# Seven block products in place of eight, over part of the columns, in the middle token stages of a fused fp32 layer

## The chip, the cores and the metric

One core of one Trainium2 chip runs one program. The metric is the time of the whole program on the device, in microseconds. Runs of this kernel agree within about 0.15%.

## The reference, cut to what matters

```python
delta = lora_B @ lora_A * 0.5
normalized = (weight + delta).reshape(O, 16, 128) / exp(scale_log)
quantized = cb[searchsorted((cb[:-1] + cb[1:]) / 2, normalized)]     # 32 levels
w_eff = (quantized * scale).reshape(O, I) + delta                    # 2048 x 2048
y = x @ w_eff.T                                                      # x: 4096 tokens x 2048
r = y @ W_base.T + b_base
probs = softmax(y @ router_w.T); ax = y @ A_w.T
mixed = einsum(einsum(ax, cores), probs)
out = x + r + (mixed @ B_w.T) * 2.0
```

Everything is fp32. The kernel multiplies the two matrices first: G = w_eff.T @ [W_base.T | A_w.T | router_w.T] + identity, 2048 x 2072, and then x @ G.

## The kernel before, in words

**Tiling.** The 2048 rows of G are 16 blocks of 128, in four groups of four. For each group there is a weight stage, which makes the group's four blocks of G in SBUF, and then a token stage, which multiplies all 4096 tokens (32 tiles `t` of 128) with them and adds the result to `part[t]`, 128 x 2072, which lives in HBM between stages. Group 0 has its own startup; the last group (`LAST` = 3) already has a token stage of another form, with pairs of tokens and seven products of half-width blocks (`ORDER`, `prod`).

**Precision.** Each product is three matmuls: both operands are split into a high part, rounded to fp32r (ScalarE copies), and a low part, the rest (a subtraction). High x high, high x low and low x high are added up in PSUM.

**Token stages 0 to 2** (`chunk`, `product`, lines 969 to 971). Token tile `t` has five chunks `c` of 384, 384, 384, 512 and 408 columns, one PSUM bank each (`m0` to `m4`), 12 matmuls a chunk. In stages 1 and 2 VectorE adds each bank to `part` (`evacuate`, line 1407), and TensorE writes a bank again when the add of the token before is done. ScalarE rounds the token's x (`xh`, line 1185), GpSimd takes its low part (`xl`, line 1623), 512 columns, in three buffers. SP loads x and part and stores part (`load_x`, `load_part` line 667, `store_part` line 672), in three buffers of part.

**The background.** Beside this, the other engines quantize the weights of later groups, half a block `q` (128 x 1024) at a time, 24 levels `j` each (`unit`): ScalarE makes a uint8 mask (line 1131, five buffers), VectorE adds it to `acc` (line 1362) and closes with the clamp, a sum of two SBUF tensors (line 1366). Seven more masks go by ScalarE (line 1137) to GpSimd (lines 1592 and 1606), which also normalises before (lines 1569, 1572; the delta rows come by DMA at level 5, and level 8 uses them) and scales after (lines 1611, 1613). Then ScalarE and GpSimd split the half block into high and low part (line 1617).

**Order.** All engines walk the same list of events (`walk`); each takes the events that are its own, in order. `Background.levels` deals the levels out between the chunks, by the share of the stage that has passed. So whatever an engine waits for holds everything behind it in the list. Stage 1 does half blocks 18 to 23, stage 2 does 26 to 31; weight stage 2 does 24 and 25.

```python
for t in range(NT):
    for c in range(NCH):
        yield ("chunk", g, t, c)
        if c == 2 and t + 2 < NT:
            yield ("x_split", g, t + 2)
        yield from back.levels(until, min(1.0, (NCH * t + c + 1) / (NT * NCH - 7)), 2 * FIRST[g + 1])
```

Of the kernel before, what the change touches and what calls it, by code (L numbers as in the profile page):

```python
# [77 lines left out]
SECOND = (506, 4)  # L78

# [8 lines left out]
    *(f"k{r}" for r in range(RING)), "x0", "x1", "x2", "pi0", "pi1", "pi2", "po0", "po1", "po2",  # L88
# [29 lines left out]
class Background:  # L118
# [29 lines left out]
def weights_of(g, back):  # L148
# [6 lines left out]
    for s in range(NS):  # L155
# [6 lines left out]
        yield from back.levels(until, min(1.0, (s + 1) / (NS - 6)), 2 * FIRST[g])  # L162
# [15 lines left out]

def operand_steps(n, k):
# [47 lines left out]
def walk():  # L227
# [11 lines left out]
class Room:  # L239
    def __init__(self, nc, ctx):  # L240
# [15 lines left out]
        self.gh = [self.take(f"gh{k}", DX, F32R) for k in range(NMAX)]  # L256
        self.gl = [self.take(f"gl{k}", DX, F32R) for k in range(NMAX)]
# [42 lines left out]
        self.tmp = self.put("tmp", at_x[0], 1536)  # L300
        row, r0 = 4 * DX, raw[0]
# [34 lines left out]
        self.chain_a, self.chain_b = (self.m[2], self.m[1], self.pd), (self.m[4], self.m[3], self.m[0])  # L336

# [256 lines left out]
def sync_program(e, R, S, io, part, delta, out):  # L594
    def raw(q):
        b, h = q // 2, q % 2
        if q >= RAW:
            wait_consumed(e, S, q - RAW)
        e.dma_start(R.wr[raw_of(q)], io["w"][b][:, h * H:(h + 1) * H]).then_inc(S[f"w{raw_of(q)}"], 16)
# [34 lines left out]
    def weight(g, s):  # L634
# [3 lines left out]
        if g == LAST and s in GUEST_LAST:  # L638
            if s == 2:
                e.wait_ge(S["used"], NS * (LAST - 1))  # L640
# [1143 lines left out]
```

## Time and profile before

| | |
|---|---|
| median of 3 runs | 2352.81 us (2351.86 to 2354.84) |
| the profiled execution | 2352.95 us, span 2351.2 us |
| PE busy | 2281.0 us, 97%, 11778 matmuls |
| VectorE / ScalarE / GpSimd busy | 1846.1 / 1464.8 / 1288.8 us |
| chain that ended last | PE 91%, DVE 6% |
| HBM | 306.41 MB read, 151.13 MB written, 195 GB/s |

PE is TensorE, DVE VectorE, ACT ScalarE, POOL GpSimd, SP the queue that issues DMAs. A matmul's duration in the trace is from its start to its modelled end, and matmuls overlap, so the pace is read from the distance of two starts. Token stage 1 runs from 891.4 to 1253.7 us, token stage 2 from 1436 to 1798 us. In a row of the timeline, the first number is the start in us and the second the duration.

### The profile page before, as it was taken

Reading aid. Unit: us, or ns where it says so; the run is one execution under the profiler, and the core shown is the slowest. Engines: PE = TensorE matmul, PEld = TensorE weight load, DVE = VectorE, ACT = ScalarE, POOL = GpSimd, SP = SyncE. Lnnn points to the kernel's source line nnn. Section 1 sums busy time; section 2 is a strip of 40 time slices with the busy share of each in tenths; the row PEclk is TensorE's granted clock in tenths of the full one; section 3 lists DMA queues with packets and bytes.
Section 4 is the critical chain, followed back from the end, with each engine's and each line's share of the span. In section 5 each row is a group of like instructions: output and inputs, shape, how many; then the busy total and the mean of one; then the engine's idle time right before and its main releaser. Section 6 shows DMA issues by size and latency. Waiting matters only on the chain.

```text
span 2351.2 us, 31846 instructions
## 1 busy us (share of the span) xinstructions
PE 2281.0 (97%) x11778; PEld 2083.8 (89%) x11778; DVE 1846.1 (79%) x2363; ACT 1464.8 (62%) x1926; POOL 1288.8 (55%) x792
## 2 busy tenths in 40 slices
PE   3989899999999999999999999999999999999999
PEld 2445479999999989999999989999999999999998
DVE  8999998889978866777777976777775666777776
ACT  8999978889877655666665665666663665121221
POOL 6888846669764336666663335666662222232331
PEclk9999999999999999999999999999999999999999
DMA  6788854453334335676674334666666666556463
GB/s 210 262 284 280 312 199 164 164 176 136 145 134 133 116 98 190 230 240 226 221 243 149 115 102 162 227 232 228 241 204 208 186 195 202 206 200 235 189 225 153
DMA packets 133088, 459.63 MB, mean 195 GB/s; under 512 B 14098, under 2 KB 66898, under 8 KB 96082
## 3 DMA queue, kind: packets, MB, share of 16 engines
q1 hardware_dynamic: 132932, 457.59, 57.3%
q8 instruction: 93, 1.52, 0.2%
q14 instruction: 63, 0.52, 0.1%
HBM read 306.41 MB, written 151.13 MB: 195 GB/s over the span
## 4 chain that ended last, share of the span: by engine, by line
PE 91%; DVE 6%; ACT 2%; DMA 1%; issue 1%; DVEq 0%; SPq 0%; ACTq 0%
PE m L970 15%; PE m L969 15%; PE m L971 15%; PE m L926 5%; PE m L927 5%; PE m L925 5%; PE m L868 5%; DVE acc L1362 4%; PE m L1018 4%; PE m L1020 4%; PE m L1019 4%; PE m L956 2%; PE m L957 2%; PE m L958 2%; ACT mk L1131 1%; PE pd L1018 1%
## 5 line engine op out<-in xcount | busy, mean ns | idle before, releaser
L1362 DVE SCALAR_TENSOR_TENSOR acc<-mk,dj,acc 128x1024 f32<-128x1024 uint8 x736 | 945.4, 1285 | 102.8 <-ACT mk L1131 83.6
L1131 ACT ACTIVATE mk<-wr,bj 128x1024 uint8<-128x1024 f32 x736 | 809.0, 1139 | 1.0 <-DVE acc L1362 0.5
L970 PE MATMUL m<-gl,xh 128*128 128x384 f32 (+2 forms) x1920 | 674.1, 351 | 0.0
L969 PE MATMUL m<-gh,xh 128*128 128x384 f32 (+2 forms) x1920 | 673.5, 351 | 0.0
L971 PE MATMUL m<-gh,xl 128*128 128x384 f32 (+2 forms) x1920 | 671.6, 350 | 0.0
L1606 POOL TENSOR_TENSOR pp<-pp,tm 128x1024 f32<-128x1024 f32 x184 | 447.3, 2431 | 22.3 <-POOL tm L1592 0.6
L971 PEld LDWEIGHTS m<-gh,xl 128*128 128x128 f32 x1920 | 360.6, 188 | 18.0
L969 PEld LDWEIGHTS m<-gh,xh 128*128 128x128 f32 x1920 | 361.0, 188 | 17.2
L970 PEld LDWEIGHTS m<-gl,xh 128*128 128x128 f32 x1920 | 360.9, 188 | 16.9
L1592 POOL TENSOR_SCALAR tm<-mp,dj 128x1024 f32<-128x1024 uint8 x192 | 217.6, 1134 | 281.5 <-ACT mp L1137 276.3
L1413 DVE TENSOR_TENSOR kl<-kw,kh 128x416 fp32r<-128x416 f32 (+3 forms) x310 | 238.0, 779 | 104.9 <-ACT kh L1165 103.7
L1165 ACT ACTIVATE kh<-kw 128x416 fp32r<-128x416 f32 (+3 forms) x310 | 169.2, 549 | 220.0 <-DMA kw<-in_wb 125.8
L1407 DVE TENSOR_TENSOR part<-m,part 128x384 f32<-128x384 f32 (+2 forms) x320 | 188.1, 588 | 139.0 <-PE m L971 138.3
L1137 ACT ACTIVATE mp<-wr,bj 128x1024 uint8<-128x1024 f32 x224 | 254.9, 1138 | 0.0
L925 PE MATMUL m<-kh,wh 128*128 128x384 f32 (+2 forms) x624 | 219.2, 351 | 0.0
L927 PE MATMUL m<-kh,wl 128*128 128x384 f32 (+2 forms) x624 | 218.6, 350 | 0.0
L926 PE MATMUL m<-kl,wh 128*128 128x384 f32 (+2 forms) x624 | 218.6, 350 | 0.0
L1185 ACT ACTIVATE xh<-xw 128x512 fp32r<-128x512 f32 x96 | 60.3, 630 | 253.2 <-DMA xw<-in_x 253.0
L868 PE MATMUL m<-rows,wr 128*128 128x384 f32 (+2 forms) x560 | 207.7, 534 | 2.7 <-DMA rows<-in_wb 2.2
L868 PEld LDWEIGHTS m<-rows,wr 128*128 128x128 f32 x560 | 112.5, 201 | 96.7 <-issue 51.3
L1454 DVE TENSOR_TENSOR part<-m,part 128x346 f32<-128x346 f32 (+1 forms) x272 | 136.0, 515 | 63.5 <-PE m L1020 30.6
L1018 PE MATMUL m<-op,pxh 128*128 128x346 f32 (+1 forms) x544 | 178.8, 329 | 0.0
(198 smaller groups left out, 3363.7 us busy)
## 6 DMA issues: line engine op xcount, KB each, us to landing
part<-part SPq DMA_DIRECT2D x192, 1036.0 KB, 7.6
rows<-in_wb SPq DMA_DIRECT2D x61, 1036.0 KB, 4.8
out<-part SPq DMA_DIRECT2D x31, 1024.0 KB, 4.5
kw<-in_ws SPq DMA_DIRECT2D x128, 208.0 KB, 2.6
xw<-in_x SPq DMA_DIRECT2D x96, 256.0 KB, 3.4
kw<-in_wb SPq DMA_DIRECT2D x92, 192.0 KB, 2.4
wr<-in_w SPq DMA_DIRECT2D x32, 512.0 KB, 8.6
dl<-delta SPq DMA_DIRECT2D x30, 512.0 KB, 5.9
```

What stands on the lines that cost most here:

```text
L868: done = e.matmul(R.m[c][:, 0:width(c)], R.wr[raw_of(q)][:, (t % 8) * 128:(t % 8 + 1) * 128], R.rows[r % 3][:, cols(c)], start=t == 0, sto ...
L925: e.matmul(bank[:, 0:w], high, kh, start=t == 0, stop=False)
L926: e.matmul(bank[:, 0:w], high, kl, start=False, stop=False)
L927: done = e.matmul(bank[:, 0:w], low, kh, start=False, stop=t == NB - 1 and not own(b, c))
L969: e.matmul(R.m[c][:, 0:w], xh, gh, start=k == 0, stop=False)
L970: e.matmul(R.m[c][:, 0:w], xh, gl, start=False, stop=False)
L971: done = e.matmul(R.m[c][:, 0:w], xl, gh, start=False, stop=stop and k == n - 1)
L1018: e.matmul(bank, high, oh, start=kp == 0 and n in (1, 2, 5), stop=False, skip_group_check=n in (3, 4, 6, 7))
L1131: e.activation(R.mk[m % NM], w, ACT.Identity, bias=R.bj[:, j:j + 1], scale=GROW).then_inc(S["mk"], 1)
L1137: e.activation(R.mp[k % 2], w, ACT.Identity, bias=R.bj[:, NV + i:NV + i + 1], scale=GROW).then_inc(S["mp"], 1)
L1362: e.scalar_tensor_tensor(R.acc, R.mk[m % NM], R.dj[:, j:j + 1], R.acc, ALU.mult, ALU.add).then_inc(S["ac"], 1)
L1606: e.tensor_tensor(R.pp, first, R.tm[scaled_level(q, i)], ALU.add).then_inc(S["pp"], 1)
```

## The change

It concerns token stages 1 and 2 (`MIXED`). The tokens are taken in 16 pairs. The first and the last pair keep their chunks; each of the 14 between is a list of 13 units (`MIX`). For the first 448 columns of each half of G (the halves are 1036 wide), the 2 x 2 block scheme of the last stage is used: two tokens by two halves of the group's rows, seven products of six matmuls of 448 columns in place of eight. The other 588 columns of each half are done as before, in three rest units a token of 392 columns, 12 matmuls each; the third takes 196 columns from each half. Products use two banks in turn, rest units the other four.

The products need sums: of G's blocks, once a stage, in pair 0 (`spread` on VectorE, eight operations of 896 columns, `spread_high` on ScalarE, `spread_low` on GpSimd), and of x, once a pair (`token_sums`, four sums of 256 columns, and `token_sums_low` on GpSimd, `token_sums_high` on ScalarE). x gets a fourth buffer. G's sums lie where `wh` was, so the half blocks of the next group are split into high and low part only in the last pair of the stage, half of the later groups' low parts on VectorE (`VECTOR_SPLITS`), and four of group 3 in its weight stage. Levels are dealt out by columns passed, none beside the first 6 units and the last 11, nor beside the first four slots of weight stage 2. The raw half block 24 is loaded in the last pair of stage 1, and normalised at its close. SP's loads and stores are issued at the events `fetch`, `more` and `half_done`. The rest of the kernel stays.

```diff
+SW = 448
+REST = (HX - SW) // 3 * 2
+MIX = (("prod", 1), ("prod", 2), ("rest", 0, 0), ("rest", 0, 1), ("prod", 6), ("prod", 5), ("rest", 0, 2), ("prod", 7),
+       ("prod", 3), ("rest", 1, 0), ("prod", 4), ("rest", 1, 1), ("rest", 1, 2))
+MIXED = (1, 2)
+MIX_FIRST, MIX_LAST = 1, PAIRS - 2
+NMIX = MIX_LAST - MIX_FIRST + 1
+SUM_SLOT = {4: 0, 6: 1, 5: 2, 3: 3}
+SPARE_RAW = {1: (3, 4, 2), 2: (0, 1, 10)}
+SPLITS = {1: tuple(range(8, 16)), 2: (16, 18, 20, 22, 17, 19, 21, 23), 3: (24, 26, 25, 27, 28, 29, 30, 31)}
+SPLIT_POS = {q: 8 * (g - 1) + k for g, qs in SPLITS.items() for k, q in enumerate(qs)}
+VECTOR_SPLITS = (17, 19, 21, 23, 25, 27)
+WAIT_LEVELS, END_LEVELS, WAIT_SLOTS = 6, 11, 4
+LATE_SPLITS = {20: 28, 24: 29, 28: 30, 32: 31}
...
-        if self.j % SPLIT_EVERY == SPLIT_EVERY - 1 and (self.q, self.j) > LAST_DELTA:
+        if self.j % SPLIT_EVERY == SPLIT_EVERY - 1 and (self.q, self.j) > LAST_DELTA and self.split < 2 * FIRST[2]:
...
-        yield from back.levels(until, min(1.0, (s + 1) / (NS - 6)), 2 * FIRST[g])
+        wait = WAIT_SLOTS if g - 1 in MIXED else 0
+        yield from back.levels(until, min(1.0, max(0, s + 1 - wait) / (NS - 6 - wait)), 2 * FIRST[g])
...
+def mixed_tokens_of(g, back):
+
+    until = UNTIL_TOKENS[g]
+    back.begin(until)
+    costs = [unit_columns(u) for u in UNITS_OF[g]]
+    unit = costs[0]
+    total, passed = sum(costs) - (WAIT_LEVELS + END_LEVELS) * unit, -WAIT_LEVELS * unit
+    for k, u in enumerate(UNITS_OF[g]):
+        p, at = u[0], k - PAIR_FIRST[g][u[0]]
+        yield ("mul", g, k)
+        if at == 0:
+            yield ("fetch", g, p)
+        if p == 0 and at in (0, 1, 2):
+            yield ("spread", g, at)
+        if p == 0 and at in (1, 2, 3, 4):
+            yield ("spread_high", g, at - 1)
+            yield ("spread_low", g, at - 1)
+        if p + 1 < PAIRS:
+            if at == 3:
+                yield ("x_split", g, 2 * p + 2)
+            if at == 4:
+                yield ("x_split", g, 2 * p + 3)
+                yield ("more", g, p)
+            if at == 5 and mixed(p + 1):
+                yield ("token_sums", g, p + 1)
+            if at == 6:
+                yield ("x_low", g, 2 * p + 2)
+            if at == 9 and mixed(p + 1):
+                yield ("token_sums_high", g, p + 1)
+                yield ("token_sums_low", g, p + 1)
+            if at == (10 if mixed(p) else 9):
+                yield ("x_low", g, 2 * p + 3)
+        elif at < 7:
+            if g + 1 < LAST or at < 4:
+                yield ("split", SPLITS[g + 1][at])
+        if at == (9 if mixed(p) else 5):
+            yield ("half_done", g, p)
+        if p == PAIRS - 1 and at == 6:
+            yield ("next_weights", g)
+        if p == PAIRS - 1 and at == 8:
+            yield ("next_rounded", g)
+        passed += costs[k]
+        yield from back.levels(until, min(1.0, max(0.0, passed / total)), 0)
+    yield ("close", g)
+    if g + 1 < LAST:
+        yield ("split", SPLITS[g + 1][7])
...
+def unit_bank(u):
+
+    if u[1] == "chunk":
+        return u[3]
+    if u[1] == "prod":
+        return 1 if u[2] in (2, 3, 5) else 0
+    return 2 + (6 * u[0] + 3 * u[2] + u[3]) % 4
+
+
+def unit_tokens(u):
+
+    if u[1] == "prod":
+        return (TARGET[u[2]][0],), {1: (0,), 2: (0,), 4: (1,)}.get(u[2], ())
+    return (u[2],), (u[2],)
...
-        for c in range(NCH):
-            wait_evacuated(e, S, g, t, c)
+        if g == 0:
+            for c in range(NCH):
+                wait_evacuated(e, S, g, t, c)
+        else:
+            e.wait_ge(S["ed"], added(g, last_unit(g, t, 0)))
...
+        elif what == "fetch":
+            g, p = at
+            if p + 1 < PAIRS:
+                load_x(g, 2 * p + 2)
+                load_x(g, 2 * p + 3)
+            if p:
+                store_part(g, 2 * p - 1)
+        elif what == "more":
+            g, p = at
+            if p:
+                load_part(g, 2 * p + 2)
+        elif what == "half_done":
+            g, p = at
+            store_part(g, 2 * p)
+            if p + 1 < PAIRS:
+                load_part(g, 2 * p + 3)
+            elif g == 1:
+                raw(2 * FIRST[LAST])
...
+            e.wait_ge(S["wl"], 8 if g == 1 else 12)
+        if s == 8 and g > 1:
+            e.wait_ge(S["wd"], 4)
...
+        if (kind, *at) == ("prod", 6):
+            e.wait_ge(S["ql"], sums_count(g, p))
+            e.wait_ge(S["bl"], 4 * g)
+        before = bank_before(g, k)
+        if before is not None:
+            e.wait_ge(S["ed"], added(g, before))
...
+        bank = (*R.m, R.pd)[unit_bank(UNITS_OF[g][k])]
+        if kind == "prod":
+            n = at[0]
+            for kp in range(2):
+                high, low = sum_factor(g, p, n, kp)
+                oh, ol = sum_operand(n, kp, False), sum_operand(n, kp, True)
+                e.matmul(bank[:, 0:SW], high, oh, start=kp == 0 and n in (1, 2, 5), stop=False, skip_group_check=n in (3, 4, 6, 7))
+                e.matmul(bank[:, 0:SW], high, ol, start=False, stop=False, skip_group_check=n in (3, 4, 6, 7))
+                done = e.matmul(bank[:, 0:SW], low, oh, start=False, stop=kp == 1, skip_group_check=n in (3, 4, 6, 7))
+        else:
+            u, i = at
+            _, xl, xh = R.token(g, 2 * p + u)
+            for b in range(GROUP[g]):
+                r = slice(b * 128, (b + 1) * 128)
+                gh, gl = rest_columns(R.gh[b], i), rest_columns(R.gl[b], i)
+                e.matmul(rest_bank(bank, i), xh[:, r], gh, start=b == 0, stop=False)
+                e.matmul(rest_bank(bank, i), xh[:, r], gl, start=False, stop=False)
+                done = e.matmul(rest_bank(bank, i), xl[:, r], gh, start=False, stop=b == GROUP[g] - 1)
+        done.then_inc(S["mc"], 1)
...
+    def token_sums_high(g, p):
+        e.wait_ge(S["qs"], 4 * sums_count(g, p))
+        if p > MIX_FIRST:
+            e.wait_ge(S["mc"], multiplied(g, prod_unit(g, p - 1, 3)))
+        elif g > 1:
+            e.wait_ge(S["used"], NS * g)
+        e.activation(R.sh[g], R.sf, ACT.Copy).then_inc(S["qh"], 1)
...
+    def mul_added(g, k):
+        p, kind, *at = UNITS_OF[g][k]
+        t = 2 * p + unit_tokens(UNITS_OF[g][k])[0][0]
+        part, bank = R.part[t % 3], (*R.m, R.pd)[unit_bank(UNITS_OF[g][k])]
+        if k == first_unit(g, t, 0):
+            e.wait_ge(S[f"pi{t % 3}"], slot_round(g - 1, t))
+        e.wait_ge(S["mc"], multiplied(g, k))
+        if kind == "chunk":
+            c = at[1]
+            to, of = part[:, cols(c)], bank[:, 0:width(c)]
+        elif kind == "rest":
+            to, of = rest_columns(part, at[1]), rest_bank(bank, at[1])
+        else:
+            first = HX * TARGET[at[0]][1]
+            to, of = part[:, first:first + SW], bank[:, 0:SW]
+            before = target_before(g, k)
+            if before is not None:
+                e.wait_ge(S["ed"], added(g, before))
+        e.tensor_tensor(to, of, to, ALU.add).then_inc(S["ed"], 1)
+
+    def split(q):
+        e.wait_ge(S["wh"], SPLIT_POS[q] + 1)
+        e.tensor_tensor(R.wl[raw_of(q)], R.wr[raw_of(q)], R.wh[high_of(q)].bitcast(F32), ALU.subtract).then_inc(S["wd"], 1)
+
+    def spread(g, k):
+        br, r, f, n = S["br"], R.sum_raw, R.sum_f, 8 * (g - 1)
+
+        def rebuilt(to, i, h):
+            e.tensor_tensor(grouped(r[to], 2), both_blocks(R.gah, i, h).bitcast(F32), both_blocks(R.gal, i, h).bitcast(F32),
+                            ALU.add).then_inc(br, 1)
+
+        if k == 0:
+            e.wait_ge(S["used"], NS * g)
+            e.wait_ge(S["lo"], NCH * FIRST[g + 1])
+            rebuilt(1, 0, 1)
+            rebuilt(0, 0, 0)
+            e.wait_ge(br, n + 2)
+            e.tensor_tensor(f[0], r[1], r[0], ALU.subtract).then_inc(br, 1)
+        elif k == 1:
+            rebuilt(2, 1, 1)
+            e.wait_ge(br, n + 4)
+            e.tensor_tensor(f[1], r[2], r[1], ALU.subtract).then_inc(br, 1)
+            e.tensor_tensor(f[2], r[2], f[0], ALU.subtract).then_inc(br, 1)
+        else:
+            rebuilt(3, 1, 0)
+            e.wait_ge(br, n + 7)
+            e.tensor_tensor(f[3], r[3], f[2], ALU.subtract).then_inc(br, 1)
...
+    def spread_low(g, k):
+        e.wait_ge(S["bh"], 4 * (g - 1) + k + 1)
+        if k in (0, 2):
+            e.wait_ge(S["br"], 8 * (g - 1) + (6 if k == 0 else 8))
+        e.tensor_tensor(R.sum_l[k], R.sum_f[k], R.sum_h[k].bitcast(F32), ALU.subtract).then_inc(S["bl"], 1)
+
+    def token_sums(g, p):
+        n, x = 4 * (sums_count(g, p) - 1), [R.token(g, t)[0] for t in (2 * p, 2 * p + 1)]
+        a11, a12, a21, a22 = (quarter(x[k // 2], 0, k % 2) for k in range(4))
+        s1, s2, s3, s4 = (grouped(R.sf[:, 256 * k:256 * (k + 1)], 2) for k in range(4))
+        for t in (2 * p, 2 * p + 1):
+            e.wait_ge(S[f"x{x_buffer(g, t)}"], x_landed(g, t))
+        if n:
+            e.wait_ge(S["ql"], n // 4)
+        if p == MIX_FIRST:
+            e.wait_ge(S["used"], NS * g)
+        e.tensor_tensor(s1, a21, a22, ALU.add).then_inc(S["qs"], 1)
+        e.tensor_tensor(s3, a11, a21, ALU.subtract).then_inc(S["qs"], 1)
+        e.wait_ge(S["qs"], n + 1)
+        e.tensor_tensor(s2, s1, a11, ALU.subtract).then_inc(S["qs"], 1)
+        e.wait_ge(S["qs"], n + 3)
+        e.tensor_tensor(s4, a12, s2, ALU.subtract).then_inc(S["qs"], 1)
+
+    def token_sums_low(g, p):
+        e.wait_ge(S["qh"], sums_count(g, p))
+        e.tensor_tensor(R.sl[g], R.sf, R.sh[g].bitcast(F32), ALU.subtract).then_inc(S["ql"], 1)
```

## Rows read from the trace of the kernel before

**Rows 1.** Windows: token stage 1; granted clock, DMA share, GB/s last.

```profile
891.40:1253.70 362.30, 362.30 (x1923) 345.20 (x1922) 275.98 (x314) 218.98 (x228) 243.67 (x141) 1.00 0.66 222
```

**Rows 2.** Waits, 895 to 1250 us: total us, times, longest.

```profile
DVE part L1407 <- PE m L971: 68.4, 120, 2.2
...
POOL wr L1569 <- DMA dl<-delta: 6.3, 4, 3.4
```

**Rows 3.** Timeline of PE, stage 1: first matmul of each run of one width.

```profile
999.66 0.40 PE L969 MATMUL m<-gh,xh 128*128 128x512 f32 x1
...
1002.45 0.34 PE L969 MATMUL m<-gh,xh 128*128 128x408 f32 x1
...
1004.68 0.34 PE L969 MATMUL m<-gh,xh 128*128 128x384 f32 x1
...
1010.97 0.40 PE L969 MATMUL m<-gh,xh 128*128 128x512 f32 x1
```

**Rows 4.** Timeline of PE, last stage: 17 intervals of 344 or 346 columns.

```profile
2101.27 0.32 PE L1018 MATMUL m<-op,pxh 128*128 128x346 f32 x1
...
2103.94 0.32 PE L1020 MATMUL m<-op,psl 128*128 128x346 f32 x1
```

**Rows 5.** Tile ps, last stage: GpSimd sums, and their low part.

```profile
L1639 POOL TENSOR_TENSOR ps<-px x16: 726/738/1098, 1918.3 to 2308.6; 128x256 f32<-128x256 f32 x16
...
L1655 POOL TENSOR_TENSOR psl<-ps,pxh x16: 2382/2394/2403, 1939.5 to 2314.5; 128x1024 fp32r<-128x1024 f32 x16
```

**Rows 6.** Groups by form, 895 to 1250 us, VectorE: busy us, mean ns.

```profile
L1362 DVE SCALAR_TENSOR_TENSOR acc<-mk,dj,acc 128x1024 f32<-128x1024 uint8 x138 | 176.9, 1282 | 14.1 <-ACT mk L1131 13.9
...
L1407 DVE TENSOR_TENSOR part<-m,part 128x384 f32<-128x384 f32 x95 | 52.8, 556 | 28.9 <-PE m L971 28.5
...
L1407 DVE TENSOR_TENSOR part<-m,part 128x512 f32<-128x512 f32 x31 | 21.4, 692 | 27.8 <-PE m L971 27.8
...
L1366 DVE TENSOR_TENSOR wr<-acc,pp 128x1024 f32<-128x1024 f32 x6 | 7.3, 1225 | 0.6
```

**Rows 7.** Timeline of VectorE, stage 1: level, add, level.

```profile
1100.73 1.29 DVE L1362 SCALAR_TENSOR_TENSOR acc<-mk,dj,acc 128x1024 f32<-128x1024 uint8 x1 [0.59 <-ACT mk L1131]
1101.93 0.55 DVE L1407 TENSOR_TENSOR part<-m,part 128x384 f32<-128x384 f32 x1
1102.40 1.28 DVE L1362 SCALAR_TENSOR_TENSOR acc<-mk,dj,acc 128x1024 f32<-128x1024 uint8 x1
```

**Rows 8.** Groups by form, 895 to 1250 us, GpSimd: low parts.

```profile
L1623 POOL TENSOR_TENSOR xl<-xw,xh 128x512 fp32r<-128x512 f32 x30 | 38.9, 1298 | 29.8 <-ACT xh L1185 29.7
...
L1617 POOL TENSOR_TENSOR wl<-wr,wh 128x1024 fp32r<-128x1024 f32 x7 | 16.9, 2412 | 1.0 <-ACT wh L1148 1.0
```

**Rows 9.** Timelines of VectorE, then GpSimd, weight stage 1.

```profile
763.20 2.12 DVE L1413 TENSOR_TENSOR kl<-kw,kh 128x384 fp32r<-128x384 f32 x1 [0.56 <-ACT kh L1165]
...
773.12 1.27 DVE L1362 SCALAR_TENSOR_TENSOR acc<-mk,dj,acc 128x1024 f32<-128x1024 uint8 x1
...
762.39 2.52 POOL L1606 TENSOR_TENSOR pp<-pp,tm 128x1024 f32<-128x1024 f32 x1
...
772.95 2.52 POOL L1606 TENSOR_TENSOR pp<-pp,tm 128x1024 f32<-128x1024 f32 x1
```

**Rows 10.** By line, 895 to 1250 us: store_part (L672), load_part (L667).

```profile
DMA to landing us min/median/max: 4.6/9.3/10.7
...
DMA to landing us min/median/max: 5.2/7.1/8.8
```

**Rows 11.** DMA issues, 895 to 1250 us: median us to landing last.

```profile
xw<-in_x SPq DMA_DIRECT2D x29, 256.0 KB, 3.4
dl<-delta SPq DMA_DIRECT2D x6, 512.0 KB, 9.3
```

**Rows 12.** Groups by form, 895 to 1250 us, ScalarE: masks, high parts of tokens.

```profile
L1131 ACT ACTIVATE mk<-wr,bj 128x1024 uint8<-128x1024 f32 x137 | 148.6, 1135 | 0.0
...
L1185 ACT ACTIVATE xh<-xw 128x512 fp32r<-128x512 f32 x30 | 19.0, 632 | 124.8 <-DMA xw<-in_x 124.8
```

More of the change, by code:

```diff
@@ L444, in wait_final_row, with mixed, units_of_stage, unit_columns @@
         e.wait_ge(S[f"f{k}"], 16)
+def mixed(p):
+    return MIX_FIRST <= p <= MIX_LAST
+def units_of_stage():
+    units = []
+    for p in range(PAIRS):
+        if mixed(p):
+            units += [(p, *u) for u in MIX]
+        else:
+            units += [(p, "chunk", u, c) for u in range(2) for c in range(NCH)]
+    return units
+def unit_columns(u):
+    if u[1] == "prod":
+        return 6 * SW
+    return 12 * (REST if u[1] == "rest" else width(u[3]))
+def unit_bank(u):
[4 more added lines that the diff above has]
+    return 2 + (6 * u[0] + 3 * u[2] + u[3]) % 4
@@ new lines, in last_unit, with first_unit, prod_unit, multiplied @@
+def last_unit(g, t, reads):
+    return max(k for k, u in enumerate(UNITS_OF[g]) if u[0] == t // 2 and t % 2 in unit_tokens(u)[reads])
+def first_unit(g, t, reads):
+    return min(k for k, u in enumerate(UNITS_OF[g]) if u[0] == t // 2 and t % 2 in unit_tokens(u)[reads])
+def prod_unit(g, p, n):
+    return PAIR_FIRST[g][p] + MIX.index(("prod", n))
+def multiplied(g, k):
+    return MC_BASE[g] + k + 1
+def added(g, k):
+    return ED_BASE[g] + k + 1
+def bank_before(g, k):
+    return max((j for j in range(k) if unit_bank(UNITS_OF[g][j]) == unit_bank(UNITS_OF[g][k])), default=None)
@@ new lines, in target_before, with sums_count, sums_free, x_buffer @@
+def target_before(g, k):
+    p, kind, *at = UNITS_OF[g][k]
+    same = [j for j in range(PAIR_FIRST[g][p], k) if UNITS_OF[g][j][1] == "prod" and TARGET[UNITS_OF[g][j][2]] == TARGET[at[0]]]
+    return max(same, default=None)
+def sums_count(g, p):
+    return NMIX * (g - 1) + p - MIX_FIRST + 1
+def sums_free(g):
+    return multiplied(g, prod_unit(g, MIX_LAST, 3))
+def x_buffer(g, t):
+    return t % 4 if g in MIXED else t % 3
+def x_landed(g, t):
+    if g == 0:
+        return 16 * (t // 3 + 1)
+    k = t % 4
+    return 16 * ((PER_SLOT[k] if k < 3 else 0) + NT // 4 * (g - 1) + t // 4 + 1)
@@ L447, in wait_evacuated, with x_released, rest_columns, rest_bank @@
+def x_released(g, k):
+    if g == 0:
+        return NCH * (3 * (PER_SLOT[k] - 1) + k + 1)
+    return multiplied(g, last_unit(g, NT - 4 + k, 1))
+def rest_columns(t, i):
+    if i < 2:
+        return t[:, HX * i + SW:HX * i + SW + REST]
+    return halves(t)[:, :, SW + REST:HX]
+def rest_bank(bank, i):
+    return bank[:, 0:REST] if i < 2 else halves(bank[:, 0:REST])
+def both_blocks(t, i, h):
+    return t.rearrange("p (a i n) -> p a i n", a=2, i=2)[:, :, i, HX * h:HX * h + SW]
 def wait_evacuated(e, S, g, t, c):
-    if g == 0 and c in ACT_CHUNKS:
+    if g in MIXED:
+        e.wait_ge(S["ed"], added(g, PAIR_FIRST[g][t // 2] + NCH * (t % 2) + c))
+    elif c in ACT_CHUNKS:
@@ L639, in weight @@
             if s == 2:
[L640 removed]
+                e.wait_ge(S["mc"], sums_free(2))
             elif s == 3:
@@ L802, in sync_program @@
                     weight(g + 1, s)
+        elif what == "fetch":
[16 more added lines that the diff above has]
+                raw(2 * FIRST[LAST])
+        elif what == "next_weights":
+            for s in range(RING):
+                weight(at[0] + 1, s)
         elif what == "close":
@@ L1084, in tensor_program @@
             chunk(*at)
+        elif what == "mul":
+            mul(*at)
         elif what == "prod":
@@ L1294, in scalar_program @@
                 weight(g + 1, 1)
+        elif what == "next_rounded":
+            weight(at[0] + 1, 0)
+            weight(at[0] + 1, 1)
+        elif what == "spread_high":
+            spread_high(*at)
+        elif what == "token_sums_high":
+            token_sums_high(*at)
         elif what == "close":
@@ L1709, in gpsimd_program @@
         elif what == "split":
-            split(*at)
+            if at[0] not in VECTOR_SPLITS:
+                split(*at)
         elif what == "slot":
```

157 lines of the change are left out of this document (123 added, 34 removed), and 3 rows, old and new, of the table COMPUTE.

## The prediction

> **What bounds the kernel now.** I read the windows by stage first, then the waits of a token stage, then the timeline of PE. Token stage 1 lasts 362.3 us with TensorE busy throughout; VectorE is busy 276.0 us, ScalarE 219.0, GpSimd 243.7 [rows 1]. Who waits says the same: VectorE waited 68.4 us for matmuls, and GpSimd 6.3 us for delta rows [rows 2]; no wait of TensorE is in that view. A busy PE isn't yet a PE at its pace, so the starts are read: 12 matmuls of 512 columns in 2.79 us, 12 of 408 in 2.23, 36 of 384 in 6.29 [rows 3], that is 0.2325, 0.186 and 0.1747 us each. A token takes 11.31 us, a pair 22.62, for 49,728 columns: 0.4549 ns a column, with next to nothing per instruction. Sixteen pairs make 361.9 us, so a token stage is its matmul columns and nothing else. That is where a saving of columns counts in full, as long as the other engines keep up.
>
> **TensorE's part.** A mixed pair has 7 products of 6 matmuls x 448 columns (18,816) and 6 rest units of 12 x 392 (28,224): 47,040 columns, 2,688 fewer, at 0.4549 ns = 1.22 us; the pair takes 21.40 us. 14 pairs in 2 stages: 28 x 1.22 = **34.2 us off**. Could the narrower matmul be held by its weight load? In the last stage 18 successive matmuls of 344 or 346 columns start over 2.67 us, 0.157 from one to the next [rows 4], under the 0.178 of 392 columns, so no. The third rest unit reads two runs of 196 columns; no row shows such a matmul. From below it costs nothing more; from above, as two of the 0.157 us just seen, 0.136 us x 24 x 28 = 91 us. I take nothing: GpSimd's sums read 128-element runs and take 0.738 us for 256 elements, in line with 2.394 for 1024 in one run [rows 5].
>
> **VectorE's part.** An add of 384 took 556 ns, of 512 692 [rows 6]; between them 448 gives 0.624 and 392 0.565. A pair has 7 x 0.624 + 6 x 0.565 = 7.76 us of adds, before 5.9. The background stays 144 levels a stage (6 half blocks x 24), at 1.282 us, with 6 clamps at 1.225 [rows 6], but now has less time: the stage has 14 x 47,040 + 2 x 49,728 = 758,016 columns, and none is issued beside the first 6 units or the last 11 of 4,608 columns, which leaves 679,680 columns, 309 us: 9.95 levels a pair. So 7.76 + 9.95 x 1.282 + 0.41 x 1.225 = 21.0 us of durations in 21.40. They overlap: an add starts 1.20 us after a level of 1.29, a level 0.47 after an add of 0.55 [rows 7], some 0.085 for each of 23 instructions: 2.0 us. Real load 19.0, spare **2.4 us** a pair. From this go the old waits for masks (13.9 of the 14.1 us ahead of the levels [rows 6], 0.9 a pair) and a new one: ScalarE rounds the next sums only when product 3 is done (one buffer), at 13.74 us of the pair (6 products of 1.22 and 3 rest units of 2.14), needs 1.1 us for it and 1.1 for the mask behind it (a mask of that size takes 1.135 [rows 12]), while VectorE wants that mask at 14.6: 1.4 us. What is left is 0.1 us. It also must not be late: a product's bank is written again after one product and one rest unit (1.22 + 2.14 = 3.4 us), where a chunk's was after four chunks (some 9 us).
>
> **GpSimd's part.** Of 243.7 us, 32 token low parts at 1.298 and 8 weight low parts at 2.412 [rows 8] are 60.8; the other 183 us are the levels' share, 1.27 us each. A mixed pair needs 9.95 x 1.27 = 12.6, two token low parts 2.6, four sums at 0.738 and their low part at 2.394 [rows 5] 5.35: 20.6 of 21.4 us. Spare **0.8 us**, a 96% load. Its products are due some 12 us after they are issued, and an engine that is late no longer waits for its inputs, so I charge little. ScalarE gets one pass of 1024 a pair and keeps a third of its time.
>
> **The port.** In weight stage 1 a subtraction of two SBUF tensors on VectorE took 2.12 us in place of some 0.55 (its PSUM sister of the same width, [rows 6]): it began at 763.20 under a GpSimd add that ended at 764.91, and ended at 765.32. The mask step (uint8 mask and accumulator, both in SBUF) began at 773.12 under another GpSimd add and took 1.27 us as ever [rows 9]. So two-tensor subtractions and adds in SBUF wait for GpSimd, levels don't. New ones of the kind are the eight rebuilt sums of 896 in pair 0 and the low parts that move to VectorE; and the clamp, which found GpSimd idle, will now find it at work. Each may wait up to 2.4 us: the clamps 0.41 x 2.4, at most 1.0 and at the middle 0.5 us a pair. With them VectorE's load and waits are 21.8 us in 21.4: I let 0.2 us a pair reach TensorE, half of the excess, since a late VectorE finds its next masks ready and waits less; nothing and 0.9 us (with 1.0 for clamps) are the ends. The Trainium skill (SBUF — State Buffer, section SBUF: two separate sides) says that the pair of ports is an exclusive lock which an operation with two SBUF inputs and a GpSimd one take in turn, and that the loser fully blocks. The trace agrees for the subtraction and not for the mask step; what it would make of this change if it held for both is the last rival.
>
> **Pair 0 and the stage ends.** The eight sums at about 1.1 us (1.225 for 1024) are 8.7 us of VectorE, beside 5.9 of adds and 5 levels (6.4): 21.0 of 22.6 us, and their low parts 4 x 2.1 on GpSimd. TensorE first wants them 6.7 us into pair 1. Cost nothing; with waits at the port VectorE runs 2 to 7 us late there, against banks of 9 us. In pair 15 eight weight halves are split after the last level: on GpSimd 4 x 2.41 = 9.6 us behind its last normalising work, on VectorE 4 x 1.2. The GpSimd ones are due at slot 0, after 22.6 us; if it is over 8 us behind, TensorE waits the rest. Raw half block 24 is loaded there ahead of the first weights: I charge 1 us a stage. In weight stage 2 48 levels go into 70 slots in place of 74, 6% denser, with the low parts of the weights prepared three slots ahead: nothing.
>
> **SP's queue.** Per pair it still moves two parts in and two out, but in another order: the odd token's load waits, at the head of the queue, for the landing of the even token's store, and the next pair's loads of x stand behind it. The store goes out when unit 8 is added, at 13.74 + 0.2 + 0.63 = 14.6 us of the pair. Stores landed in 4.6 to 10.7 us, median 9.3, loads in 5.2 to 8.8, median 7.1 [rows 10], but those went out together with each other and with x. This store goes out alone, so I take 5 us: the load leaves at 19.6 and lands near 25 to 27, due at 30.8 (end of the sixth unit of the next pair). Then x (3.4 us [rows 11]) isn't late either. The delta rows for the next half block are asked for at level 5 and used at level 8, 6.5 us on, and take 9.3 [rows 11]; twice in six they fall behind that wait. This lands on GpSimd's 0.8 us, and its lateness hides part of it.
>
> **Sum.** -34.2 + 28 x 0.2 + 2 x 1 at the stages' ends = -26.6 us. The profiled execution took 2352.95 us (span 2351.2), 0.14 over the median of the runs shown: 2352.8 - 26.6 = 2326.2, say **2326 us**. Ends of this case: the whole 34.2, 2318.6, and 0.9 us a pair lost, 2346.
>
> **Rivals.** (a) *GpSimd becomes the bound.* If its waits for delta (6.3) and a like sum at other handovers stay beside a 96% load (spare 14 x 0.8 = 11 us a stage), levels finish late, clamps hold VectorE, and adds hold TensorE: some 5 to 10 us a stage, 2336 to 2346. For it: the load. Against: those waits were of an engine that had run ahead. (b) *The store is slow, and the change is slower.* With S us for the even token's store, x leaves at 14.6 + S, and the first mask behind it needs 3.4 us to land and 0.63 + 1.13 for x's high part and the mask [rows 12], due at 26.7 (the third unit's add of the next pair): VectorE stalls for S - 6.9. It has 2.4 us to spare and 1.2 were gained, so with no other wait the kernel loses from S = 10.5 on, and with the 1.4 us behind product 3 from 9.1 on; at the longest store seen, 10.7, that is 3.8 + 1.4 - 2.4 = 2.8 us x 28 - 34.2 = +44, 2397; at the median of 9.3, 1.4 x 28 - 34.2 = +5, 2358. For it: the median of 9.3. Against: nothing else large is in flight by then. (c) *VectorE's lateness isn't made up.* If the waits for masks, clamps and x add up in full and a level in progress delays adds past the 3.4 us of a bank, 1.2 us a pair go: 2353, no change. (d) *Levels block at the port too.* 12.8 us of levels and 20.6 of GpSimd in turn would take 33 us a pair, 28 x 12 = 330 us slower, 2650. By that rule token stage 1 would have had 176.9 + 243.7 us in 362, so it's all but excluded.
>
> **Chances.** Likeliest 0.62, (a) 0.18, (b) 0.11, (c) 0.08, (d) 0.01. 0.2% is 4.7 us, about what this kernel's runs can tell from no change. Faster: the first two, 0.80; same 0.08; slower 0.12. Range 2318 to 2347: it holds the likeliest case and (a), and leaves (b), (c) and (d) out.
>
> **What would show it.** Right: matmuls of 448 start 0.204 us apart, of 392 0.178, those with two runs as well; a token stage takes 345 to 351 us; TensorE's waits there stay under 6 us; VectorE busy 88% or more, GpSimd 93% or more inside the pairs. Wrong: matmuls of the first product units waiting for part, a wait of part or xh for DMA of microseconds in each pair, clamps of 3 us, a stage of 356 us or more, or the third rest unit above 0.2 us a matmul.

## The result and the profile after

The changed kernel took **2357.81 us** (median of 20 runs, 2354.79 to 2362.82), the kernel before 2352.65 on the same chip (20 runs, 2351.29 to 2356.02): a ratio of 1.0021, 95% interval 1.0015 to 1.0028. It is slower by 0.2%, where 2326 was forecast and 2318 to 2347 given. From the start of one stage's first matmul to the next stage's:

| us | before | after |
|---|---|---|
| startup and token stage 0 | 336.7 + 373.2 | 334.2 + 373.2 |
| weight stage 1, token stage 1 | 181.8, 362.0 | 181.7, **361.6** |
| weight stage 2, token stage 2 | 181.7, 362.0 | 182.3, **362.3** |
| weight stage 3, last token stage | 185.0, 368.9 | **189.0**, 369.2 |

By its columns a token stage would take 14 x 21.39 + 2 x 22.62 = 344.7 us. So the two stages gave back 16.9 and 17.6 us, all that 34.2 us of fewer columns had brought, and weight stage 3 lost 4.0 more. Of the profile's page, the share of each engine and the chain that ended last, of which PE was 91% before:

```profile
PE 2254.3 (96%) x11610; PEld 2061.6 (88%) x11610; DVE 1918.7 (82%) x2469; ACT 1496.8 (64%) x1962; POOL 1439.8 (61%) x934
...
PE 71%; DVE 8%; POOL 6%; DMA 6%; ACT 5%; issue 3%; SPq 0%; POOLq 0%; DVEq 0%; ACTq 0%
```

The windows of token stage 1 and of 912 to 1215 us in it, which holds pairs 1 to 13 (913.2 to 1206.7) and the start of pair 14 (us, then busy time and count of PE, weight loads, DVE, ACT, POOL, then clock, DMA share, GB/s), for [rows 1]:

```profile
891.40:1255.00 363.60, 349.15 (x1846) 334.11 (x1845) 307.85 (x368) 233.13 (x242) 315.36 (x210) 1.00 0.60 221
912.00:1215.00 303.00, 289.01 (x1526) 277.12 (x1527) 257.67 (x315) 207.16 (x213) 277.44 (x190) 1.00 0.63 232
```

TensorE, busy throughout before, now idles 14 us in this stage. In the pairs' window GpSimd is busy 277.4 of 303 us (92%) and VectorE 257.7 (85%): neither is full. The waits in that window (total, times, longest), for [rows 2]:

```profile
ACT sh L1503 <- POOL sf L2031: 50.2, 10, 8.0
DVE acc L1687 <- ACT mk L1435: 42.2, 23, 5.1
ACT xh L1491 <- DMA xw<-in_x: 33.3, 9, 7.7
PE m L1270 <- DVE part L1747: 12.8, 10, 2.5
ACT sh L1503 <- PE m L1272: 12.2, 3, 5.1
```

Where VectorE waited for TensorE, TensorE now waits for VectorE, at L1270, the first product of a pair. VectorE waits for masks, and ScalarE, which makes them, for GpSimd's sums of x (`sf`) and for x itself. One pair shows how these hang together. It starts at 1028.87, the next at 1052.10: 23.23 us in place of 21.39. Timelines of GpSimd, ScalarE, VectorE and TensorE:

```profile
1042.95 0.74 POOL L2026 TENSOR_TENSOR sf<-xw 128x256 f32<-128x256 f32 x1
...
1045.16 0.74 POOL L2031 TENSOR_TENSOR sf<-xw,sf 128x256 f32<-128x256 f32 x1
...
1037.91 2.18 ACT L1435 ACTIVATE mk<-wr,bj 128x1024 uint8<-128x1024 f32 x2
1045.93 1.06 ACT L1503 ACTIVATE sh<-sf 128x1024 fp32r<-128x1024 f32 x1 [5.84 <-POOL sf L2031]
1046.90 1.13 ACT L1435 ACTIVATE mk<-wr,bj 128x1024 uint8<-128x1024 f32 x1
...
1042.86 1.15 DVE L1747 TENSOR_TENSOR part<-m,part 128x448 f32<-128x448 f32 x2
1048.07 1.29 DVE L1687 SCALAR_TENSOR_TENSOR acc<-mk,dj,acc 128x1024 f32<-128x1024 uint8 x1 [4.07 <-ACT mk L1435]
...
1051.34 0.61 DVE L1747 TENSOR_TENSOR part<-m,part 128x448 f32<-128x448 f32 x1
...
1052.10 0.44 PE L1270 MATMUL m<-gh,xh 128*128 128x448 f32 x1 [1.60 <-DVE part L1747]
```

GpSimd comes to the four sums 14.1 us into the pair and ends them at 1045.90. ScalarE had reached the rounding at 1040.1 and stood 5.84 us; the mask behind it, which doesn't need the sums, came at 1048.0. VectorE stood 4.07 us for that mask, so it added the pair's last product, whose matmuls had begun at 1044.83, only at 1051.34; TensorE, which writes that bank first in the next pair, stood 1.60 us. Each engine hands on a part of its lateness.

### The profile page after: what moved, and what is told of

Its sections match the earlier page's. It is cut to its first block, busy times and chain, and to the rows that moved or that the text cites. A ratio compares the mean times of both kernels' runs of the same rounds, so it can differ in the third digit from the quotient of the medians.

```text
span 2353.6 us, 31902 instructions
## 1 busy us (share of the span) xinstructions
PE 2254.3 (96%) x11610; PEld 2061.6 (88%) x11610; DVE 1918.7 (82%) x2469; ACT 1496.8 (64%) x1962; POOL 1439.8 (61%) x934
## 4 chain that ended last, share of the span: by engine, by line
PE 71%; DVE 8%; POOL 6%; DMA 6%; ACT 5%; issue 3%; SPq 0%; POOLq 0%; DVEq 0%; ACTq 0%
PE m L1106 7%; PE m L1214 6%; PE m L1213 6%; PE m L1215 6%; PE m L1165 5%; PE m L1167 5%; PE m L1166 5%; DVE acc L1687 4%; PE m L1320 4%; PE m L1322 4%; PE m L1321 4%; ACT mk L1435 3%; DMA xw<-in_x 2%; PE m L1200 2%; PE m L1201 2%
## 5 line engine op out<-in xcount | busy, mean ns | idle before, releaser
L1781 DVE TENSOR_TENSOR kl<-kw,kh 128x416 fp32r<-128x416 f32 (+3 forms) x310 | 254.5, 833 | 97.0 <-ACT kh L1470 96.2
L1214 PE MATMUL m<-gl,xh 128*128 128x384 f32 (+2 forms) x800 | 280.9, 351 | 0.0
L1213 PE MATMUL m<-gh,xh 128*128 128x384 f32 (+2 forms) x800 | 280.6, 351 | 0.0
L1215 PE MATMUL m<-gh,xl 128*128 128x384 f32 (+2 forms) x800 | 279.8, 350 | 0.0
L1747 DVE TENSOR_TENSOR part<-m,part 128x448 f32<-128x448 f32 (+4 forms) x362 | 209.7, 591 | 22.5 <-PE m L1215 16.3
L1320 PE MATMUL m<-op,pxh 128*128 128x346 f32 (+1 forms) x544 | 178.9, 329 | 0.0
L1321 PE MATMUL m<-op,pxh 128*128 128x346 f32 (+1 forms) x544 | 174.2, 320 | 0.0
L1280 PE MATMUL m<-gl,xh 128*128 128x392 f32 x504 | 171.9, 341 | 0.0
L1279 PE MATMUL m<-gh,xh 128*128 128x392 f32 x504 | 171.9, 341 | 0.0
L1281 PE MATMUL m<-gh,xl 128*128 128x392 f32 x504 | 171.5, 340 | 0.0
```

What stands on the lines that cost most here:

```text
L1213: e.matmul(R.m[c][:, 0:w], xh, gh, start=k == 0, stop=False)
L1214: e.matmul(R.m[c][:, 0:w], xh, gl, start=False, stop=False)
L1215: done = e.matmul(R.m[c][:, 0:w], xl, gh, start=False, stop=stop and k == n - 1)
L1320: e.matmul(bank, high, oh, start=kp == 0 and n in (1, 2, 5), stop=False, skip_group_check=n in (3, 4, 6, 7))
L1321: e.matmul(bank, high, ol, start=False, stop=False, skip_group_check=n in (3, 4, 6, 7))
```

## The experiments

Three theories were set against each other. **H**, head of the line: `token_sums_high` stands too early in the common list, and ScalarE holds the masks while it waits for GpSimd's sums. **X**: the loads of x land late, and ScalarE's `xh` holds the masks. **G**: GpSimd's load is the bound, wherever things stand. The expectations name a fourth, **B**: the two banks of the products are written again too soon for a loaded VectorE. Each run was timed beside the kernel before on the same chip, and the brackets give the ratio to it with its interval; the edits are made to the changed kernel. Medians of different groups of runs were taken on different chips, where the kernel before took 2351.2 to 2353.9 us, so a difference of 2 or 3 us between such medians tells nothing by itself.

**Where the rounding stands.** `round11` moves the sums' rounding and their low part two units later, to unit 11; `round12` has 12 in its place; `round11_low9` moves the rounding alone.

```diff
-            if at == 9 and mixed(p + 1):
+            if at == (11 if mixed(p) else 9) and mixed(p + 1):
                 yield ("token_sums_high", g, p + 1)
                 yield ("token_sums_low", g, p + 1)
```

> The rounding of the next pair's sums (ScalarE) and their low part (GpSimd) go two units later, behind unit 11 instead of unit 9. Theory H (ScalarE is held: it stands in its order before the rounding until GpSimd's late sums are there, the masks behind it come late, VectorE's adds come late and TensorE waits for a bank at each pair's start): VectorE's waits for masks in the mixed pairs fall from 4 us a pair to under 2, and the program takes 2325 to 2338 us. Rival G (GpSimd's load of 96% is the bound whatever the order): within 5 us of 2357. Rival B (two banks for products are reused too soon for a loaded VectorE): within 5 us of 2357.

> Only ScalarE's rounding of the sums goes behind unit 11; GpSimd's low part stays at its old place behind unit 9, so GpSimd may stand for ScalarE. Theory H: still faster than the change, 2325 to 2345 us, since ScalarE runs ahead of VectorE and reaches the rounding before GpSimd, which is late, gets to the low part. Rival G: within 5 us of 2357. Rival B: the same. If it is slower than the kernel with both moved, GpSimd's waits for ScalarE count.

> Rounding and low part both behind unit 12, the pair's last. Theory H: the mask side is as good as behind unit 11 or better, but the low part is due at the fifth unit of the next pair, 6.7 us later, and a GpSimd that is 6 us late makes TensorE wait for it: 2328 to 2350 us, with waits of product 6 for the low part of the sums in the trace. Rival G and rival B: within 5 us of 2357.

Measured: **2342.23** (0.9954, 0.9937 to 0.9971), **2343.32** (0.9962, 0.9947 to 0.9977) and **2351.49** (0.9995, 0.9985 to 1.0004). The place of the rounding is worth 15.6 us, with no less work for GpSimd and the same banks, so H holds and neither G nor B is the whole cause; the low part's own place doesn't count. H alone asked for more: 2342.23 lies above its 2325 to 2338, though VectorE's waits for masks did fall from 3.2 us a pair to 1.8. At unit 12, just above the 2350 expected, most of the gain is lost again. The product that needs the sums is the fifth unit of the next pair, and TensorE's waits for their low part rise from 3.9 us in round11 to 7.1 over the two stages, as expected; in the traces these stages are 2.0 and 1.8 us longer, and the rest of the 9.3 us isn't accounted for. The waits of round11 in the same window, then its timeline of ScalarE, VectorE and SP:

```profile
ACT xh L1492 <- DMA xw<-in_x: 62.3, 14, 7.4
DVE acc L1688 <- ACT mk L1436: 23.9, 19, 3.0
ACT sh L1504 <- POOL sf L2032: 23.8, 10, 6.6
```

```profile
986.22 0.63 ACT L1492 ACTIVATE xh<-xw 128x512 fp32r<-128x512 f32 x1 [7.33 <-DMA xw<-in_x]
...
987.93 1.29 DVE L1688 SCALAR_TENSOR_TENSOR acc<-mk,dj,acc 128x1024 f32<-128x1024 uint8 x1 [3.00 <-ACT mk L1436]
...
978.86 0.32 SPq L884 DMA_DIRECT2D part<-part  x1
979.22 0.91 SPq L877 DMA_DIRECT2D xw<-in_x  x2
980.52 0.33 SPq L892 DMA_DIRECT2D part<-part  x1
```

The waits for sums halve and those for x double, to 62.3 us: the same 3 us stall of VectorE, now behind x. x leaves at 979.2, behind the odd token's load of `part` and ahead of a store, 1 MB each, and is used at 986.2.

**GpSimd's share.** `thin_sums` takes the four sums of x over 16 of 256 columns from the second mixed pair on: they take 0.9 us in place of 2.95, so GpSimd has some 2 us a pair less; the rest of the sums is left out, and the order is that of the change.

```diff
+        if p > MIX_FIRST:
+            a11, ..., s4 = (v[:, :, 0:8] for v in (a11, ..., s4))
```

> From the second mixed pair on the four sums of x are taken over 16 of 256 columns each; the rest of the sums is left out, everything else stays at its place. That takes about 2 us a pair off GpSimd, 10% of its load, and brings the sums sooner. Theory H: GpSimd makes up its lateness, ScalarE isn't held, 2322 to 2335 us. Rival G: the same, 2322 to 2335; this run and the one behind unit 11 together tell the two apart. Rival B: within 5 us of 2357.

Measured: 2343.83 (0.9962, 0.9947 to 0.9977), 14 us better and a miss: H and G both asked for 2322 to 2335. Less work on GpSimd and a later rounding cure the same wait, and both stop near 2343, which left X as the next cause.

**The loads of x.** `round11_xeven` sends the even token's x half a pair earlier, ahead of the load of `part` that waits for a store. `round11_sp` does this and also moves the odd part's load behind x. `sp_only` has these loads with the rounding back at unit 9. `round11_sp_thin` is round11_sp with the thin sums, part of them again left out.

```diff
             if p + 1 < PAIRS:
-                load_x(g, 2 * p + 2)
+                if p == 0:
+                    load_x(g, 2)
                 load_x(g, 2 * p + 3)
...
             store_part(g, 2 * p)
+            if p + 2 < PAIRS:
+                load_x(g, 2 * p + 4)
             if p + 1 < PAIRS:
                 load_part(g, 2 * p + 3)
```

> On top of the rounding behind unit 11, the even token's x is loaded at unit 9 of the pair before (its buffer is free since unit 6), ahead of the odd part's load; the odd token's x stays at the pair's start. Theory X (what is left of the loss is x: ScalarE stands before x's high part for 7 us, since the 256 KB land in 6.3 us in place of the 3.4 of the kernel before, behind and beside two transfers of part, and the masks behind it come 3 us late): most of it goes, 2328 to 2337 us, against 2342. Rival G (the rest is GpSimd's load): within 4 us of 2342. Rival B (the rest is the short reuse of the product banks): within 4 us of 2342.

> As the run before, and the odd token's part is loaded at the next pair's start, behind x and ahead of the store, so that nothing large is in flight when x is. Theory X: 2326 to 2335 us, VectorE's waits for masks under 1 us a pair. Against it stands that the part is then 5 us nearer to its first add, 9.2 us into the pair: should it land in over 8.5 us, VectorE waits for part in the trace and the gain is gone. Rivals G and B: within 4 us of 2342.

> Only the loads as in the run before, with the rounding left at its old place behind unit 9. Theory H says that the two causes stand one behind the other on the same two engines (ScalarE's order and VectorE's wait for masks): 2338 to 2350 us, so each alone gives 10 to 18 of the 39 us. If x were the only cause this run alone would reach 2332; if the rounding were, it would stay at 2357.

> Both moves, and the four sums of x over 16 of 256 columns each from the second mixed pair on (the rest of the sums is left out): 2 us a pair less for GpSimd. It prices what GpSimd's load still costs once nobody stands for it. Theory H with X: within 4 us of the run with both moves and whole sums, so GpSimd's 96% is harmless by itself. Rival G: 6 us or more faster than that run, down to 2320 to 2324.

Measured: **2330.63** (0.9897, 0.9882 to 0.9912), 2331.52 (0.99, 0.9886 to 0.9915), 2346.85 (0.9969, 0.9959 to 0.998) and **2326.87** (0.988, 0.9866 to 0.9895). The loads alone are worth 11 us, the rounding alone 15.6, both 27; part's own load adds nothing. The first three fell where H and X expected them. Waits of round11_xeven from 912 to 1215 us, as above (its pairs 1 to 13 run from 916.1 to 1196.7), and a window of 281 us, the length of 13.1 undisturbed pairs:

```profile
ACT sh L1507 <- POOL sf L2035: 40.0, 10, 7.1
ACT xh L1495 <- DMA xw<-in_x: 29.5, 13, 4.8
...
DVE acc L1691 <- ACT mk L1439: 9.1, 9, 2.5
```

```profile
912.00:1193.00 281.00, 278.12 (x1477) 268.18 (x1476) 253.67 (x305) 201.08 (x206) 269.44 (x188) 1.00 0.67 241
```

ScalarE still stands 40 us for the sums, and it costs VectorE 9.1: what counts is not how long ScalarE stands but which masks it holds. GpSimd works 269.4 of 281 us (96%), more densely than in the changed kernel, and TensorE loses 2.6 us over 13 pairs (10 of them within 0.1 us of 21.39). So G is no bound, and B isn't either, with the same two banks. GpSimd's load keeps a share: with thin sums (round11_sp_thin against round11_sp) it fell to 248.0 of 281 us and 4.7 us went, between the 4 at most that H expected and the 6 or more of G. In the traces 1.8 and 2.0 us of it are in the two token stages, most of that in pair 9 (23.1 to 21.39 us).

**The last weight stage and the spacing of levels.** `late_vector` is round11_xeven with the four late low parts on VectorE; `late_apart` spaces these over slots 24, 28, 40 and 44 besides (a slot is one of the 160 steps of that stage); `all_gpsimd` is round11_xeven with every low part on GpSimd; `early_levels` is late_vector with levels from behind the second unit of the stage, not the sixth.

```diff
-VECTOR_SPLITS = (17, 19, 21, 23, 25, 27)
+VECTOR_SPLITS = (17, 19, 21, 23, 25, 27, 28, 29, 30, 31)   # late_vector; () in all_gpsimd
-LATE_SPLITS = {20: 28, 24: 29, 28: 30, 32: 31}
+LATE_SPLITS = {24: 28, 28: 29, 40: 30, 44: 31}             # late_apart
-WAIT_LEVELS, END_LEVELS, WAIT_SLOTS = 6, 11, 4
+WAIT_LEVELS, END_LEVELS, WAIT_SLOTS = 2, 11, 4             # early_levels
```

> On top of the rounding behind unit 11 and the early even x: the four late low parts in the last weight stage (28 to 31) go from GpSimd to VectorE. Theory L (while GpSimd takes them, VectorE's low parts of the weights wait at the shared port, up to 2.2 us in place of 0.58, and TensorE waits for them: this stage took 189.0 us where the kernel before took 185.0): the stage takes 185 to 186 us again, and the program 2326 to 2329 against 2330.6. Rival (the four extra roundings on ScalarE make the weights late): the stage stays at 188 to 189.

> On top of the rounding behind unit 11 and the early even x (2330.6): all late low parts of weights on GpSimd, which undoes the change's 'half on VectorE'. Eight at 2.41 us are 19.3 us, behind GpSimd's last scaling (4.3 us) and its lateness, for a slot 8 due 22.6 + 18 us after pair 15 began; only the first four are due at slot 0. Theory L: VectorE's low parts of the weights wait at the port for more of them, 1 to 4 us slower than 2330.6. Rival: they are hidden, within 1 us.

> As the run before, with levels from the third unit of a token stage on instead of the seventh (WAIT_LEVELS 6 to 2), so beside the preparation of the sums: undoes the change's first half of 'no levels beside their preparation'. Theory G' (GpSimd at 96% is still 6 us late in the middle pairs, and spreading the levels over 3% more time helps): 2 to 4 us off in pairs 5 to 9. Against it: in pair 0 eight sums of 1.1 us, five more levels and the waits at the port come together, so pair 1 may start late. I expect the two to cancel within 2 us.

> As the kernel with the four late low parts on VectorE (2327.6), which are now taken at slots 24, 28, 40 and 44 of the last weight stage instead of 20, 24, 28 and 32. What is left of that stage's loss (187.3 us against 185.0) should be the collision of the split at slot 20 with the operands that ScalarE and VectorE form at slots 17 to 21: the stage then takes 185.5 to 186.5 us and the program 2326 to 2327.5. If the stage stays above 187 us, the rest of its loss has another cause, which stays open.

Measured: 2327.56 (0.99, 0.9886 to 0.9913), 2331.33 (0.9911, 0.9896 to 0.9927), **2336.31** (0.9935, 0.9922 to 0.9947) and 2328.45 (0.9893, 0.9876 to 0.9909). The last weight stage took 188.8 us in round11_xeven, 187.3 in late_vector (185 to 186 expected), 186.4 in late_apart (185.5 to 186.5 expected, but the program at 2327.5 at most) and 189.6 in all_gpsimd, against 185.0 before. Between late_vector and late_apart the totals tell no difference, nor do they between round11_xeven and late_vector, whose ratios are 0.9897 and 0.99: the 1.5 us is read from the stage alone. Giving half of the low parts to VectorE moves nothing in the token stages, which took 348.6 and 348.7 us in all_gpsimd, 348.7 and 348.9 in round11_xeven; the last weight stage is 0.8 us longer without it, and the totals don't settle between the 1 to 4 us of theory L and its rival. early_levels was expected to cancel within 2 us and cost 8.75: each token stage is 3.5 or 3.8 us longer. Its waits of TensorE, 885 to 1800 us:

```profile
PE m L1274 <- POOL xl L2012: 6.0, 2, 3.0
PE m L1217 <- DVE part L1751: 2.7, 4, 0.8
```

GpSimd, given levels beside the eight sums of pair 0, is 3.0 us late with the low part of x for pair 1, 1.4 in the other versions. Pair 0 with its handover takes 27.6 us there, 24.1 in the other versions, and pairs 1 and 2 lose some 2 us more. Pairs 5 to 9 do gain what the theory said, 1.8 us a stage (all five take 21.39). So the gap without levels, which I had only counted as lost room, is worth some 3.6 us a stage, net.

## Why the prediction was wrong

**TensorE's part held.** Timeline of PE in the pair shown above:

```profile
1030.17 0.37 PE L1270 MATMUL m<-gh,xh 128*128 128x448 f32 x1
...
1031.40 0.34 PE L1279 MATMUL m<-gh,xh 128*128 128x392 f32 x1
...
1035.66 0.36 PE L1270 MATMUL m<-th,sh 128*128 128x448 f32 x1
...
1038.09 0.34 PE L1279 MATMUL m<-gh,xh 128*128 128x392 f32 x1
...
1040.24 0.36 PE L1270 MATMUL m<-th,sh 128*128 128x448 f32 x1
```

Six matmuls of 448 take 1.23 us (0.204 each), 24 of 392 take 4.26 (0.178), and the 12 of a third rest unit, with two runs of 196, at 1038.09, 2.15 (0.179). An undisturbed pair takes 21.38 to 21.39 us, where 21.40 was forecast. The 34.2 us were really there. That two runs cost nothing was luck, since I took it from rows of GpSimd, which show nothing of TensorE.

**The step that failed is GpSimd's part**: "its products are due some 12 us after they are issued, and an engine that is late no longer waits for its inputs, so I charge little". I had its load right (20.6 us a pair; 269.4 us in 13.1 undisturbed pairs are 20.5) and asked when TensorE needs the sums. But ScalarE needs them first, at its place in the list, and stands in order: what it holds isn't the sums' rounding, which has time, but masks, which have none. VectorE's part saw this wait and charged it 1.4 us, for product 3 alone; the wait for product 3 was 12.2 us in 3 pairs, that for GpSimd 50.2 in 10. A later place for the rounding gave back 15.6 us.

**Second, SP's queue**: "Then x (3.4 us) isn't late either". The landings of x (L876), load_part (L883) and store_part (L891) from 912 to 1215 us, for [rows 10, 11]:

```profile
DMA to landing us min/median/max: 3.2/5.6/7.4
...
DMA to landing us min/median/max: 4.6/4.8/5.8
...
DMA to landing us min/median/max: 3.8/4.1/8.7
```

The stores landed in 4.1 us, those of the even tokens, rival (b)'s, in 3.8 to 5.7, near the 5 that I took, and the load in 4.8, so rival (b) fell with its slow store. The late x that it foresaw came by another way: x goes out between a load and a store of 1 MB, and took 5.6 us in the median and 7.4 at most, where I had kept the 3.4 of a kernel that issued them in another order. I had bounded the store from both sides and x from none. Sending the even x earlier gave back 11.6 us (round11 to round11_xeven), and x landed in 4.7 us in the median there, in place of 6.1 to 6.3. GpSimd's waits for delta rows, which I had put behind that queue and into rival (a), didn't come: there is none in either token stage.

**VectorE's lateness adds up.** I let 0.2 us a pair reach TensorE, "since a late VectorE finds its next masks ready". It did not find them: ScalarE was late too. Measured: 15.5 and 16.2 us over 13 pairs a stage, 1.2 a pair. That is the size of rival (c), to which I gave 0.08, and a product's bank is the one in the waits, as it said; that the sizes agree is partly luck, since its waits for clamps didn't come. Rival (a) foresaw GpSimd's lateness; its price of 5 to 10 us a stage is about what the rounding's place gave back (15.6 us over two stages), but its reason, a 96% load, isn't the cause by itself: round11_xeven has that load and loses 2.6 us over 13 pairs.

**The stage ends.** I charged nothing for pair 0 and 1 us a stage for pair 15. Pair 15 took its 22.61 us, and pair 0 with its handover cost 1.4 us, which is TensorE's wait for the low part of x for pair 1: right in size by luck. Weight stage 3 was charged nothing and lost 4.0 us. With the four low parts on VectorE 1.5 us of it came back, and 0.9 more with these spaced, so GpSimd's low parts are shown as the cause of a part only. TensorE's waits in that stage after (1.4 us in 4 before):

```profile
PE m L1200 <- DVE kl L1781: 4.8, 6, 1.3
```

The same wait is 4.4 us in round11_xeven, 3.4 in late_vector and 2.0 in late_apart, so it follows the stage; of the 1.4 us by which late_apart's stage is still over 185.0 it holds 0.6, and the rest stays open.

**By the sum:** 34.2 gained, less 31.7 between the mixed pairs, 2.8 at pair 1's start and 4.6 in weight stages 2 and 3, is 4.9 us slower; the medians differ by 5.2. (The two profiled spans differ by 2.4: the startup of this execution was 2.4 us shorter.) The versions with both orders mended that compute all that the reference does reach 2327.6 to 2331.5, the forecast's own region. late_vector (2327.56) is some 30 us under the changed kernel and 1.0% under the kernel before.

## What to carry to other kernels

When a product passes through several in-order engines, ask of each engine on the way when it comes to wait, and what stands behind it that isn't part of the product: the due time at the end of the path says nothing of that. Give a blocking step the latest place that its consumer allows, and try the neighbouring places, since two units were worth 15.6 us and a third lost 9. Price a small load by what is issued around it in the new order; and count a gap without background work as what it protects, not only as room lost.

## What the runs showed of the hardware

I had `acc` in SBUF. It lies in PSUM (`bank("acc", 2)`), so a level and a clamp each have one SBUF input, not two, and the part on the port read the mask step wrongly. Timeline of VectorE and GpSimd after: three spreads and a clamp, then `kl` in weight stage 3 with TensorE's wait for it:

```profile
896.26 1.08 DVE L1771 TENSOR_TENSOR tf<-tr,tf 128x896 f32<-128x896 f32 x1
...
897.73 2.83 DVE L1757 TENSOR_TENSOR tr<-gh,gl 128x896 f32<-128x896 f32 x1
900.59 2.89 DVE L1775 TENSOR_TENSOR tf<-tr,tf 128x896 f32<-128x896 f32 x1
...
897.49 5.05 POOL L2014 TENSOR_TENSOR tl<-tf,th 128x896 fp32r<-128x896 f32 x2 [18.95 <-DVE tf L1771]
...
956.15 1.23 DVE L1691 TENSOR_TENSOR wr<-acc,pp 128x1024 f32<-128x1024 f32 x1
...
955.46 2.40 POOL L2035 TENSOR_TENSOR sl<-sf,sh 128x1024 fp32r<-128x1024 f32 x1
...
1821.03 0.58 DVE L1781 TENSOR_TENSOR kl<-kw,kh 128x416 fp32r<-128x416 f32 x1
...
1822.60 2.23 DVE L1781 TENSOR_TENSOR kl<-kw,kh 128x416 fp32r<-128x416 f32 x1 [0.70 <-ACT kh L1470]
...
1822.00 2.38 POOL L2000 TENSOR_TENSOR wl<-wr,wh 128x1024 fp32r<-128x1024 f32 x1 [38.39 <-ACT wh L1453]
...
1824.88 0.46 PE L1200 MATMUL m<-kh,wh 128*128 128x416 f32 x1 [1.30 <-DVE kl L1781]
```

The spreads, with two SBUF inputs, take 2.83 and 2.89 us under GpSimd's subtractions, in place of 1.08; `kl` takes 2.23 in place of 0.58. The clamp takes its 1.23 under a GpSimd subtraction as it did beside an idle GpSimd [rows 6], and all 14 clamps from 889 to 1796 us take 1.22 to 1.23, four of them under such a subtraction, so the 0.5 us a pair that I charged for it was nothing. The Trainium skill (SBUF — State Buffer, section SBUF: two separate sides) ties the lock to two SBUF inputs; with `acc` where it lies, every row shown here agrees with it, the levels too (1.27 to 1.29 us, all 322 in both token stages and the weight stage between), and rival (d) had no ground. Of the weight low parts on VectorE the trace has three in token stage 1, at 2.1 us in the mean, so VectorE spent nearly GpSimd's own time on them.
